# Linear layer of a four-layer block: the residual started in the output bank, and the output product as three fp32r passes

## The reference, cut to what matters

```python
X = layernorm(x)                       # per token
QKV = X @ W_in.T + b_in
Q, K, V = split(QKV)
Q, K = rope(Q), rope(K)                # first 128 of 256 features
A = sum over tokens of (K / max(|K|, 1e-12)) * V
Y = (A * Q) @ W_out.T + b_out
x = x + (Y + X)                        # residual of the layer is X, the normed x
```

## Time and profile before

| | us |
|---|---|
| median of three runs | 576.86 (575.9 to 577.86) |
| profiled execution | 577.33 |
| its span, first to last instruction | 575.4 |
| TensorE matmuls busy | 562.1 (98%) |
| VectorE busy | 468.0 (81%) |
| ScalarE busy | 371.1 (64%) |
| GpSimd busy | 220.6 (38%) |

### The profile page before, as it was taken

The page is one execution under the profiler, slowest core; times in us unless marked ns, Lnnn a source line. Parts: engine busy times, 40 slices in busy tenths (PEclk is TensorE's granted clock), DMA queues, the critical chain, the costliest instruction groups (busy, mean ns, idle before and its releaser), DMA issues.

```text
span 575.4 us, 12867 instructions
## 1 busy us (share of the span) xinstructions
PE 562.1 (98%) x4131; PEld 531.4 (92%) x4131; DVE 468.0 (81%) x1475; ACT 371.1 (64%) x1037; POOL 220.6 (38%) x324
## 2 busy tenths in 40 slices
PE   8999999999999999999999999999999999999995
PEld 8899999999999999999999999999998888888884
DVE  5888789778878997797789778878887999778875
ACT  5987556656755756576566557756976777654452
POOL 3782224233322422332233233322447789603320
PEclk9999999999999999999999999999999999999998
DMA  8806000000000000000000000000000000001001
GB/s 332 290 1 229 2 2 2 1 1 0 0 0 0 0 0 0 0 0 0 0 0 0 0 0 0 0 0 1 2 1 1 1 2 1 2 0 38 27 32 55
DMA packets 9152, 14.71 MB, mean 26 GB/s; under 512 B 1568, under 2 KB 6688, under 8 KB 9120
## 3 DMA queue, kind: packets, MB, share of 16 engines
q1 hardware_dynamic: 9120, 14.30, 7.1%
HBM read 12.20 MB, written 2.10 MB: 25 GB/s over the span
## 4 chain that ended last, share of the span: by engine, by line
PE 86%; DVE 6%; POOL 3%; ACT 3%; issue 1%; DVEq 0%; POOLq 0%
PE bank L655 68%; PE bank L741 5%; PE bank L757 5%; PE bank L760 2%; PE bank L665 2%; PE bank L870 1%; PE bank L933 1%; ACT prob L1147 1%; PE bank L946 1%; PE bank L1054 1%; POOL qkv L473 1%; DVE raw L1791 1%; POOL prob L513 0%; ACT big L1120 0%; DVE xn L1758 0%
## 5 line engine op out<-in xcount | busy, mean ns | idle before, releaser
L526 POOL TENSOR_SCALAR prob<-prob,rowinv 128x256 f32<-128x256 f32 (+1 forms) x127 | 96.1, 769 | 268.5 <-DVE rowinv L1572 268.5
L655 PE MATMUL bank<-xT,big 128*128 128x256 f32 x984 | 129.7, 284 | 0.1
L655 PEld LDWEIGHTS bank<-xT,big 128*128 128x128 f32 x984 | 123.4, 192 | 1.0 <-issue 0.2
L1147 ACT ACTIVATE prob<-prob,negmax 128x128 f32<-128x128 f32 (+1 forms) x256 | 112.9, 446 | 8.1 <-DVE negmax L1556 8.1
L655 PE MATMUL bank<-wp,oT 128*128 128x256 f32 x768 | 102.5, 283 | 0.4 <-DVE oT L1502 0.3
L655 PEld LDWEIGHTS bank<-wp,oT 128*128 128x128 f32 x768 | 96.8, 190 | 1.4 <-DVE oT L1502 0.8
L1109 ACT ACTIVATE qT<-bank 128x512 fp32r<-128x512 f32 x68 | 40.6, 597 | 72.8 <-PE bank L655 72.1
L655 PE MATMUL bank<-pT,v 128*128 128x512 f32 (+1 forms) x384 | 79.8, 343 | 0.7 <-DVE pT L1502 0.5
L655 PEld LDWEIGHTS bank<-pT,v 128*128 128x128 f32 x384 | 63.2, 189 | 9.7 <-issue 1.0
L1502 DVE TENSOR_TENSOR pT<-bank,pT 128x512 fp32r<-128x512 f32 (+1 forms) x128 | 65.1, 550 | 3.0 <-ACT pT L1109 3.0
L1109 ACT ACTIVATE pT<-bank 128x512 fp32r<-128x512 f32 (+1 forms) x128 | 55.2, 483 | 12.1 <-PE bank L757 10.0
(11 more groups left out here) (186 smaller groups left out, 962.0 us busy)
## 6 DMA issues: line engine op xcount, KB each, us to landing
raw<-in_wq SPq DMA_DIRECT2D x4, 512.0 KB, 6.8
raw<-in_wp SPq DMA_DIRECT2D x4, 512.0 KB, 7.3
x<-in_x SPq DMA_DIRECT2D x7, 256.0 KB, 6.9
out<-x SPq DMA_DIRECT2D x7, 256.0 KB, 2.1
raw<-in_w_gu SPq DMA_DIRECT2D x2, 640.0 KB, 4.9
raw<-in_w_in SPq DMA_DIRECT2D x1, 768.0 KB, 4.8
raw<-in_w_down SPq DMA_DIRECT2D x1, 640.0 KB, 6.5
raw<-in_wk SPq DMA_DIRECT2D x1, 512.0 KB, 3.9
```

The lines of the kernel that those rows point to most:

```text
L526: m = pool.tensor_scalar(prob[:, j % 2, 0, a:b], prob[:, j % 2, 0, a:b], rowinv[:, j % 2, r:r + 1], None, ALU.mult)
L655: m = pe.matmul(out, lhs(a), rhs(b), start=first and i == 0, stop=last and i == len(passes) - 1, skip_group_check=True)
L1147: m = act.activation(prob[:, j % 2, i, a:b], prob[:, j % 2, i, a:b], ACT.Exp, scale=-1.0, bias=negmax[:, 2 * i + r:2 * i + r + 1], accum_o ...
```

## The change

- yT moves from `raw` to `pT0`, the attention's transposed probabilities, and gets a high and a low half. `linear_y` on ScalarE writes the high part (fp32r); VectorE's new `linear_y_lo` computes Q times A once more and subtracts the high part.
- w_out gets high and low parts in `big`, where the attention's V weights were: `late_layer_hi(OUT)` on ScalarE and the new `out_weights_lo` on VectorE, each once, ahead of the linear loop.
- `linear_out` makes 12 fp32r matmuls through `mm3` that add onto what the bank holds.
- `linear_residual` on ScalarE writes the normed x into bank Y, with the same scale and bias; x itself stays as it was. It is placed ahead of `weigh`, and waits for the bank addition of the batch before.
- GpSimd's `linear_bias` goes. VectorE's `linear_add` computes bank plus the row b_out into x, in place of `add_bank`.

```diff
-        lin_out = raw_out.rearrange("p (k n) -> p k n", k=KT)
-        yT = rawf[:, 1536:2048].rearrange("p (k s) -> p k s", k=KT)
+        lin_out = big[:, 4 * 512:6 * 512].rearrange("p (a k n) -> p a k n", a=2, k=KT)
+        yT = pT0[:, :, :].rearrange("p a (k s) -> p a k s", k=KT)
...
# GpSimd
                 if n > 1:
-                    pool.wait_ge(s_ly, 2 * n - 2)
+                    pool.wait_ge(s_lylo, n - 1)
                 pool.tensor_tensor(q_sb[n % 2][:, 0, :].rearrange("p (t s) -> p t s", t=ST), q_cos, q_sin, ALU.add).then_inc(s_lqr, 1)
...
-            def linear_bias(n):
-                wait_apart(pool, s_lres1, n + 1)
-                add_row(n, 1).then_inc(s_lres, 1)
...
# TensorE
             def linear_out(n):
-                pe.wait_ge(s_ly, 2 * n + 2)
+
+                pe.wait_ge(s_lylo, n + 1)
                 if n == 0:
-                    pe.wait_ge(s_rawl[1], 48)
-                    pe.wait_ge(s_ya, NB)
-                else:
-                    pe.wait_ge(s_la, n)
+                    pe.wait_ge(s_outlo, 1)
+                pe.wait_ge(s_lres, n + 1)
                 for t in range(ST):
                     for k in range(KT):
-                        m = pe.matmul(bY[:, t * D:(t + 1) * D], yT[:, k, t * P:(t + 1) * P], lin_out[:, k, :],
-                                      start=t + k == 0, stop=t + k == 2, skip_group_check=True)
+                        m = mm3(pe, bY[:, t * D:(t + 1) * D], lambda a: yT[:, a, k, t * P:(t + 1) * P],
+                                lambda a: lin_out[:, a, k, :], False, t + k == 2)
...
# ScalarE, batch 7 of the attention
                             linear_x_hi(1, 1)
-                            linear_residual(0)
+                            late_layer_hi(OUT)
...
             def linear_residual(n):
-                act.wait_ge(s_ln, n + 1)
+                act.wait_ge(s_lrs, n + 2)
+                act.wait_ge(*((s_la, n) if n > 0 else (s_ya, NB)))
                 for t in range(ST):
-                    xs = x[:, bass.ds(ST * n + t, 1), :].rearrange("p o d -> p (o d)")
-                    m = act.activation(xs, xs, ACT.Identity, bias=l_scale[:, 1, ST * n + t:ST * n + t + 1],
-                                       scale=l_scale[:, 0, ST * n + t:ST * n + t + 1])
-                m.then_inc(s_lres1, 1)
+                    at = ST * n + t
+                    m = act.activation(bY[:, t * D:(t + 1) * D], x[:, at:at + 1, :].rearrange("p o d -> p (o d)"), ACT.Identity,
+                                       bias=l_scale[:, 1, at:at + 1], scale=l_scale[:, 0, at:at + 1])
+                m.then_inc(s_lres, 1)
...
             def linear(n):
                 linear_x_hi(n + 1, (n + 1) % 2) if n + 1 < NB else gated_x_hi(0)
                 if n > 1:
                     k_squares(n)
+                if n < NB - 1:
+                    linear_residual(n - 1)
                 weigh(n)
                 linear_y(n - 1)
                 linear_q(n)
...
                 if n == NB - 1:
                     gated_x_hi(1)
-                if n < NB - 1:
-                    linear_residual(n + 1)
+                    linear_residual(n - 1)
...
             gated_silu(0, 0)
             linear_y(NB - 1)
+            linear_residual(NB - 1)
             hidden_hi(0, 0)
...
# VectorE
+            def out_weights_lo():
+                src, (high, low), _ = LAYER_WEIGHTS[OUT]
+                lo(low, src, high, (s_lwhi, OUT + 1), s_outlo)
+
+            def linear_y_lo(n):
+                for e in range(2):
+                    dve.wait_ge(s_ly, 2 * n + e + 1)
+                    m = dve.scalar_tensor_tensor(yT[:, 1, e, :], q_sb[n % 2][:, e, :], A_sb[:, e:e + 1],
+                                                 f32(yT[:, 0, e, :]), ALU.mult, ALU.subtract)
+                m.then_inc(s_lylo, 1)
...
+            def linear_add(n):
+
+                dve.wait_ge(s_lo, n + 1)
+                dve.tensor_tensor(x[:, ST * n:ST * (n + 1), :], bY[:, :].rearrange("p (t d) -> p t d", t=ST),
+                                  biases[:, 1:2, :].to_broadcast([P, ST, D]), ALU.add).then_inc(s_la, 1)
...
             def linear(n):
                 if n > 1:
                     linear_apply(n + 1) if n + 1 < NB else gated_apply(0)
+                    linear_y_lo(n - 2)
                     q_products(n - 1)
...
                     if n < NB - 1:
-                        add_bank(n - 2, bY, s_lo, s_lres, s_la)
+                        linear_add(n - 2)
                         linear_x_lo(n + 1, (n + 1) % 2)
...
             linear_apply(2)
+            out_weights_lo()
             add_y(NB - 1)
...
             gated_x_lo(1)
+            linear_y_lo(NB - 2)
             linear_sum(NB - 1)
             q_products(NB - 1)
-            add_bank(NB - 2, bY, s_lo, s_lres, s_la)
+            linear_add(NB - 2)
             dve.wait_ge(s_gn, 2)
             ln_moments(NB + 1, 2)
             hidden_tile(0, 0)
+            linear_y_lo(NB - 1)
             hidden_tile(0, 1)
             gated_apply(2)
             hidden_lo(0, 0)
-            add_bank(NB - 1, bY, s_lo, s_lres, s_la)
+            linear_add(NB - 1)
```

28 lines of the change are left out of this document (14 added, 14 removed).

## The result

The changed kernel is slower. Its median is 582.01 us (seven executions, 578.96 to 582.87) against 576.72 us (seven, 575.22 to 577.86) for the kernel before beside it; the ratio is 1.0073 [1.0055, 1.0091], some 4.2 us. The medians themselves are 5.3 us apart: the executions of the changed kernel lie in two groups, three at 578.96 to 579.3 and four at 582.01 to 582.87, and the median is one of the upper group. So I go by the ratio. Forecast were +2.6 us and 579.4; the median lies on the upper end of the range, 582.0. The same kernel ran again later, beside the first experiments: 1.0064 [1.005, 1.0078], 580.42 us.

A forecast was written before the change was run, and what follows sets the result against it. VectorE was taken to bound the kernel until weigh(7), then TensorE. y_lo's 5.1 less 3.75 us of blocks gave +1.35, the end +1.25: +2.6 us, 579.4 us against the median 576.86, range 575.6 to 582.0.

The forecast's parts named there:

- Part 1: Output product on TensorE: 12 fp32r matmuls for 4 fp32 ones, about 0.1 us less per batch, 0.1 us counted in all.
- Part 2: y_lo on VectorE: 0.85 us a pair, six pairs in linear(2) to linear(7), 5.1 us into the full engine.
- Part 3: GpSimd's row additions go: the VectorE instructions they block give back 3.75 us together.
- Part 4: Residual by ScalarE into bank Y ahead of weigh, and y pipelined deeper: counted at nothing, with hardly any cover left.
- late transposes: TensorE's transposes and token sums shift 1.3 to 1.6 us behind y_lo: counted at nothing, 0.3 us each if cover lacks.
- gaps on VectorE: Sign of being wrong: gaps in VectorE's cycles would mean the loop or y_lo's inputs pace it.
- Part 5: End of the linear layer: batch 6's product waits for y_lo(6), +1.35 us, less 0.1 for the product, +1.25 us.
- y_lo(7) "adds nothing": At the end, the first two gate tiles, 4.02 us, cover y_lo(7), so nothing is added.
- The blocks go almost entirely, and y_lo is short: Rival on VectorE: y_lo at 0.68 us, relief of 4.5 us; +0.7 us, 577.6, no change; chance 0.27.
- TensorE paces: Rival: TensorE paces cycles 4 and 5, product drops 0.4 us eight times; -2.2 us, 574.7; chance 0.16.
- The residual becomes the loop: Rival: ScalarE's residual ahead of weigh makes a 7.0 us loop, five cycles lose 0.3 to 0.5 each; 581.5; chance 0.14.

The follow-up runs named there:

- e3: Changed kernel with the fp32 product of before, no y_lo and no w_out split, so only the residual's move; 0.9983 of the kernel before, 576.29 us.
- f1: Changed kernel without y_lo, the same 12 matmuls made from y's high part alone; 0.9965 of the kernel before, 574.91 us.
- e4: Changed kernel with residual in x and GpSimd's row additions as before, so only the three-pass product and y_lo; 1.0179 of the kernel before, 588.16 us.
- f2: Changed kernel with y_lo computed but neither read nor awaited by TensorE, same 12 matmuls from the high part; 1.006 of the kernel before, 579.92 us.
- e2: Changed kernel with TensorE's transposes placed ahead of the output product of batch n-2; 1.0053 of the kernel before.
- f4: Changed kernel with y_lo(6) ahead of gated_x_lo(1) on VectorE and residual(6) ahead of gated_x_hi(1) on ScalarE; 1.0061 of the kernel before.
- g2_end: Changed kernel with batch 5's bank addition and batch 6's residual early, and y_lo(6) ahead of gated_x_lo(1); 1.0068 of the kernel before.
- g1_residual_end: Against e3: batch 5's bank addition right behind k_cosine(7), batch 6's residual ahead of weigh(7); 0.997 of the kernel before, 575.15 us.

## Why the prediction was right, and where it fell short

The direction and the place were right; the size was too small: +2.6 us told, +3.5 in the profiles, +3.7 and +4.2 by the two ratios. That the sum came that near is in part luck. Taken in the order before, e3, f1, changed, the computation splits into three steps:

| step | forecast | measured |
|---|---|---|
| the residual's move (before to e3) | -3.75 | -0.94 |
| the product in fp32r (e3 to f1) | -0.1 | -0.95 |
| y_lo (f1 to changed) | 5.1 + 1.35 = +6.45 | +5.39 |
| together | +2.6 | +3.50 |

Each step is off by 0.85 us or more, and the errors mostly cancel. In another order the steps would differ, as e4 shows: they are not additive. The forecast counted each block and each pair as if VectorE alone set the pace; e3 regains 2.22 us of the blocks in the five cycles, where TensorE is then full in two, and loses 1.06 at the end.

**Part 1, the product.** Too small: 0.1 us told, 0.95 measured (f1 against e3). It is covered in the cycles, as told (0.12 us in five), but not behind them. The reading took the 1.54 us from the product's start to the gate product's as the fp32 product's price. The gate product behind an fp32 one also takes longer: e3 and f1 differ by 0.10 us in the product and by 0.30 with the gate product behind it. The changed kernel has part of that too, the 0.34 us that its gated layer gains. The Trainium skill (FP8 and Floating Point Precision, TensorE Precision Notes) counts four passes for true fp32; by that rule three would save a quarter, of the 1.82 us ahead of transposes an estimate of some 0.45. The trace shows 0.28 there (1.82 to 1.54).

**Part 2, y_lo.** 0.79 us a pair in place of 0.85, and 4.74 for six in place of 5.1. f2 against f1 prices the same pairs at 3.66 in the six cycles: without them VectorE would have waited here and there, in f1 0.32 us twice for `linear_q`.

**Part 3, the blocks.** Told 3.75, measured 3.40 (0.96, 0.60, 0.64, 0.37, 0.83). The one term that failed is `ternary_apply` of batch 7, 0.5: it took 1.25 us before and after. The row addition (L460, 451.47 to 452.76) reached only 0.08 us into it; beside it ran `q_rotate`, before (L490) and after (L493):

```profile
452.68 1.25 DVE L1736 TENSOR_SCALAR y<-x,ternary_moments,ternary_rstd 128x256 f32<-128x256 f32 x2
452.73 0.73 POOL L490 TENSOR_TENSOR qkv<-raw 128x256 f32<-128x256 f32 x1
453.39 0.73 POOL L493 TENSOR_TENSOR qkv<-raw 128x256 f32<-128x256 f32 x1 [2.02 <-DVE raw L1806]
```

That the block is `q_rotate`'s is read from these times alone; no run moves it. Parts 2 and 3 leave 4.74 - 3.40 = +1.34; the two errors cancel, +1.35 was told.

**Part 4 failed,** in the sentence on the late transposes ("Counted at nothing; if a cycle lacks the cover, 0.3 us each"). Until `k_copy(7)` the loss is 0.80 + 1.39 = 2.19 us, and of the 0.85 that the blocks and pairs don't give, 0.75 are VectorE's new idle time in the five cycles (1.91 us, against 1.16). Follow the changed kernel's timelines from the third stretch into the fourth. TensorE gets y_lo at 476.1 and its transposes run at 477.71. ScalarE's copy of them waits:

```profile
478.35 0.60 ACT L1104 ACTIVATE xT<-bank 128x512 fp32r<-128x512 f32 x1 [1.92 <-PE bank L661]
478.84 0.41 ACT L1339 ACTIVATE raw<-qkv 128x256 f32<-128x256 f32 x1
...
480.87 0.91 ACT L1346 ACTIVATE prob<-xn_b,prob 128x256 f32<-128x256 f32 x2 [0.18 <-POOL prob L516]
```

Behind that copy stand, on ScalarE's queue, `k_squares` (L1339) and `weigh` (L1346). I had checked who needs the transposes on VectorE, not what stands behind their copy on ScalarE. In GpSimd's timeline `k_inverse` (L512) waits for the squares, and releases `weigh`:

```profile
479.82 0.22 POOL L512 TENSOR_SCALAR k_bound<-k_norm 128x2 f32<-128x2 f32 x1 [0.39 <-ACT raw L1339]
480.12 0.71 POOL L516 TENSOR_TENSOR prob<-k_bound,exponent 128x2 f32<-128x2 f32 x1
```

`weigh` releases `linear_apply` at 481.92, after 0.47 us of idle VectorE, and behind that stands the next y_lo. So there is a loop: y_lo, product, transposes, copy, squares, GpSimd, `weigh`, `linear_apply`, y_lo. It is what the prediction named as a sign of being wrong, gaps on VectorE. f2 cuts the loop at TensorE's wait and gets back 0.68 us in the five cycles; e2 cuts it at the transposes and gets back 0.28, with a fallen clock in the way.

**Part 4, the residual,** at nothing in the cycles: right in the third and fourth cycle, where ScalarE still waits 0.18 us for GpSimd ahead of `weigh`. In the others the residual ends with GpSimd's result or behind it, in the fifth by 0.5 us, and there VectorE did not wait for `weigh`. At the end it was not right (next point).

**Part 5, the end.** Told +1.25, measured +1.65. The wait for y_lo(6) is there, 1.14 us, with the releaser as told; 1.32 us are added between the start of `gated_x_lo(1)` and the product, near the 1.35 told, and 0.34 come from a later `gated_x_lo(1)`, behind a later `weigh(7)` through the loop above (e2 took off 0.32). What I had not seen is the layer below: with y_lo gone, the residual of batch 6 costs 0.8 (f1: 8.17 against 7.37) to 1.06 us (e3). The 0.4 us between them in the forecast made it look harmless, and hid it. y_lo(7) "adds nothing": true only as long as y_lo(6) is late (f4).

**The rivals.** "The blocks go almost entirely, and y_lo is short": y_lo fell between, but `apply(4)`, `apply(7)` and `ternary_apply` kept 1.68, 1.51 and 1.25 us. "TensorE paces": TensorE does pace some cycles once VectorE is relieved, but the product gave 0.95 us in all and not 3.2, and y_lo cost more than that. "The residual becomes the loop": no, though another loop of the same kind and price did.

**What stays open.** Four of the first seven executions took 582.01 to 582.87 us, with a mean granted clock of 0.993 to 0.995, the others 578.96 to 579.3 with 0.997 to 0.999. The clock's fall behind the gap of 2.2 us, seen in the profile of g2_end at a cost of 1.6 us and a mean clock of 0.993, would make such a group. This is argued, not shown: no profile of the changed kernel itself caught it, and filling the gaps did not settle it. What the lower clock adds to the times of e4_product_only is not separated either.

**The better version.** g1_residual_end keeps the half of the change that pays, and is 0.3% faster than the kernel before: 0.997 [0.9956, 0.9983], 575.15 against 576.84 us.

## What to carry to other kernels

When a result passes through one more operation on a full queue, add up two prices: its start-to-start time there, and for every engine that now waits for it, what stands behind that wait in order, on that queue and on the queues of those that it feeds. Removing a long GpSimd operation is worth the VectorE instructions that it blocks, not its own time, and what moves up in its place blocks too; what is held back can block the next instruction instead. Take a change of two halves apart before judging it: here one gained 0.2% (0.3% with its end mended) and the other lost more than that. And when the instruction behind a changed one is of another kind, compare the distance to the one after it as well.
